# Products of keys, scores and carried keys split into 64-column halves in one stretch, and the result turned behind the third token product

## What is computed

```
z = cumlogsumexp(s);  g = exp(z_prev - z);  p = exp(s - z)
hk = hk * g + k (x) p;   ok = q @ hk;   pv = softmax(ok)      # one 64x64 state per head
hv = hv * g + p (x) v;   ov = pv @ hv                         # one 64x128 state per head
o  = ov * rsqrt(mean(ov^2) + eps) * g_norm * silu(x @ Wg);  out = o @ Wo
```

## Time and profile before

| | |
|---|---|
| median of 3 runs | 1312.45 us (1312.39 to 1312.88) |
| the profiled execution | 1312.18 us, span 1310.5 us |
| TensorE busy | 1301.9 us, 99% |
| VectorE, ScalarE, GpSimd busy | 71%, 41%, 33% |
| a cell, from the turn of `k` to the next (cell 13, 474.92 to 510.50 us) | 35.58 us |

### The profile page before, as it was taken

One profiled execution on the slowest core, in us unless ns is written; L12 is line 12 of the kernel. 1 busy time (PEld: TensorE's weight loads), 2 busy tenths in 40 slices (PEclk: granted clock), 3 DMA queues, 4 the chain that ended last, 5 costly groups with the idle time before them and its releaser, 6 DMA issues.

```text
span 1310.5 us, 21956 instructions
## 1 busy us (share of the span) xinstructions
PE 1301.9 (99%) x8644; PEld 1150.5 (88%) x8644; DVE 934.2 (71%) x1887; ACT 534.5 (41%) x1551; POOL 426.4 (33%) x390
## 2 busy tenths in 40 slices
PE   9999999999999999999999999999999999999998
PEld 7888888888988888888888888888888898988886
DVE  6777777777777777777777677777777777767654
ACT  5634443344334443444334434444334434632221
POOL 4412342154223431234225422343123413442211
PEclk9999999999999999999999999999999999999999
DMA  7002100010000100010001000010000110000000
GB/s 239 27 33 82 33 17 2 1 57 17 1 1 25 33 17 2 25 33 17 1 1 55 8 13 2 25 33 18 1 25 25 65 34 1 1 1 33 33 33 33
DMA packets 20023, 36.04 MB, mean 28 GB/s; under 512 B 3024, under 2 KB 3024, under 8 KB 19920
## 3 DMA queue, kind: packets, MB, share of 16 engines
q1 hardware_dynamic: 19920, 34.63, 8.1%
HBM read 30.43 MB, written 4.19 MB: 26 GB/s over the span
## 4 chain that ended last, share of the span: by engine, by line
PE 99%; DVE 1%; issue 0%; ACT 0%; POOL 0%; POOLq 0%; DVEq 0%
PE p L1059 15%; PE p L1060 15%; PE p L1061 15%; PE t L1144 5%; PE o L1328 3%; PE s L1212 3%; PE xb L1281 3%; PE p L1212 2%; PE o L1264 2%; PE t L1328 2%; PE o L1266 2%; PE s L1155 2%; PE s L1636 2%; PE s L1156 2%; PE s L1157 2%; PE s L1637 2%
## 5 line engine op out<-in xcount | busy, mean ns | idle before, releaser
L1059 PE MATMUL p<-wvg_hi,xt_hi 128*128 128x512 f32 x508 | 201.5, 397 | 0.0
L1060 PE MATMUL p<-wvg_lo,xt_hi 128*128 128x512 f32 x508 | 198.5, 391 | 0.0
L1061 PE MATMUL p<-wvg_hi,xt_lo 128*128 128x512 f32 x508 | 197.9, 390 | 0.0
L554 POOL TENSOR_TENSOR orstd<-ovar,minus_half 128x8 f32<-128x8 f32 x32 | 52.4, 1637 | 424.8 <-DVE ovar L1010 424.8
L516 POOL TENSOR_TENSOR s_lo<-sums,s_hi 128x512 fp32r<-128x512 f32 x64 | 83.0, 1298 | 225.9 <-ACT s_hi L645 225.9
L1059 PE MATMUL p<-xt_hi,wsqk_hi 128*128 128x512 f32 x376 | 149.4, 397 | 0.0
L1060 PE MATMUL p<-xt_lo,wsqk_hi 128*128 128x512 f32 x376 | 146.9, 391 | 0.0
L1061 PE MATMUL p<-xt_hi,wsqk_lo 128*128 128x512 f32 x376 | 146.6, 390 | 0.0
L620 ACT ACTIVATE v_tok<-p 128x256 f32<-128x256 f32 x128 | 49.6, 387 | 220.8 <-PE p L1061 217.8
L908 DVE COPY hv<-xb 64x128 f32<-64x128 f32 x192 | 55.1, 287 | 89.4 <-PE xb L1281 88.1
L1061 PEld LDWEIGHTS p<-wvg_hi,xt_lo 128*128 128x128 f32 x508 | 95.4, 188 | 20.7
(11 more groups left out here) (284 smaller groups left out, 3549.9 us busy)
## 6 DMA issues: line engine op xcount, KB each, us to landing
raw<-in_Wvg SPq DMA_DIRECT2D x32, 256.0 KB, 2.7
raw<-in_Wsqk SPq DMA_DIRECT2D x24, 256.0 KB, 2.7
raw<-in_L_attn_Wo SPq DMA_DIRECT2D x16, 256.0 KB, 2.9
acc<-in_x SPq DMA_DIRECT2D x4, 1024.0 KB, 5.7
out<-acc SPq DMA_DIRECT2D x16, 256.0 KB, 2.0
acc<-in_x_turned SPq DMA_DIRECT2D x3, 1024.0 KB, 8.8
acc<-in_x_turned SPq DMA_DIRECT2D x4, 256.0 KB, 4.1
v_raw<-in_L_ffn_V SPq DMA_DIRECT2D x1, 1024.0 KB, 5.5
```

The costliest lines, as they stand in the source:

```text
L554: nc.gpsimd.tensor_tensor(orstd[:], ovar[:], minus_half[:], ALU.pow).then_inc(orstd_done, 1)
L1059: nc.tensor.matmul(out_, lh, rh, start=(k == 0), stop=False)
L1060: nc.tensor.matmul(out_, lh, rl, start=False, stop=False)
L1061: last = nc.tensor.matmul(out_, ll, rh, start=False, stop=(k == n - 1))
```

## The change

1. `running_keys`, the scores' products and the carried keys' products are made per head, with 64 columns of weights and the result in its own 64 partitions of the bank. The products of `ok` are swapped: `e_tok` and `hk` are now the weights and `ws_t` and `q_t` move, so `ok` comes out with slots on partitions.
2. They stand in one stretch. The turns of `rz_t` are gone, both turns of `y` stand ahead of it.
3. `ok` is scaled by `rz_t` (`okt`), turned by TensorE behind token product 2 into the bank `s1`, and VectorE reads it there for the largest and the subtraction. `pz` is turned unscaled, and VectorE scales it by `rz_t` on the way to `pz_t`. ScalarE's copies to `rz_tok` and `pz_t` are gone.
4. On VectorE `add_m24(1)` and `add_m1` still stand behind the subtraction. ScalarE and GpSimd make `e_tok_hi`, `e_tok_lo` and `v_lo` ahead of the parts of `sums`.

```diff
@@ cell_tensor
-                nc.tensor.matmul(XB[:, 0:P], k_tok[:, c, :], e_tok[:, c, 1:3, :].rearrange("p h m -> p (h m)"),
-                                 start=(c == 0), stop=True, skip_group_check=True).then_inc(hk_summed, 1)
+                for h in range(2):
+                    mm = nc.tensor.matmul(XB[h * DK:(h + 1) * DK, h * M:(h + 1) * M], k_tok[:, c, h * DK:(h + 1) * DK],
+                                          e_tok[:, c, 1 + h, :], start=(c == 0), stop=True, skip_group_check=True)
+                mm.then_inc(hk_summed, 1)
+            def slots_of_scores(c):
+                for h in range(2):
+                    nc.tensor.matmul(OB[h * M:(h + 1) * M, tokens(c)], e_tok[:, c, 1 + h, :], ws_t[:, c, h, :],
+                                     start=(c == 0), stop=True, skip_group_check=True)
+            def slots_of_carried(c):
+                pe.wait_ge(hk_kept, cell.count(CH - 1, c))
+                for h in range(2):
+                    mm = nc.tensor.matmul(OB[h * M:(h + 1) * M, tokens(c)], hk[:, c - 1, h * M:(h + 1) * M],
+                                          q_t[:, tokens(c)], start=False, stop=True, skip_group_check=True)
...
             token_proj(pe, cell, 2)
+            pe.wait_ge(ok_scaled, cell.count(1, 1))
+            turned(OK_BANK, [okt[:, tokens(c)] for c in range(CH)], ok_turned)
             running_values(0)
...
-            pe.wait_ge(pz_done, cell.count(1, 1))
-            turned(PZ_BANK, [pz[:, c, :, :].rearrange("p h m -> p (h m)") for c in range(CH)], pz_turned)
+            pe.wait_ge(exp_done, cell.count(1, 1))
+            turned(PZ_BANK, [ok[:, c, :, :].rearrange("p h m -> p (h m)") for c in range(CH)], pz_turned)
@@ cell_vector
+            if not first(cell):
+                y_sums(dve, cell, 0)
+                add_m24(dve, cell, 0)
+                y_sums(dve, cell, 1)
             dve.wait_ge(ok_summed, cell.count(1, 1))
+            nc.vector.tensor_tensor(okt[:], OB[:], rz_t[:], ALU.mult).then_inc(ok_scaled, 1)
+            dve.wait_ge(ok_turned, cell.count(1, 1))
+            nc.vector.tensor_reduce(top[:], by_token, AX_X, ALU.max).then_inc(top_done, 1)
...
+            nc.vector.tensor_tensor(groups, by_token,
                                     top[:].rearrange("p (g a) -> p g a", a=1).broadcast_to([P, 2 * CH, M]),
                                     ALU.subtract).then_inc(ok_less_top, 1)
...
                 add_m24(dve, cell, 1)
                 add_m1(dve, cell)
...
+            dve.wait_ge(pz_turned, cell.count(1, 1))
+            nc.vector.tensor_tensor(pz_t[:], PZ_BANK[:], rz_t[:], ALU.mult).then_inc(pz_t_done, 1)
```

More of the change, by code:

```diff
@@ L297, in attention @@
         k_tok = sb("k_tok", [P, CH - 1, P])
[L298 removed]
+        okt = sb("okt", [P, T])
         hk = sb("hk", [P, CH - 1, P])
         ok = sb("ok", [P, CH, 2, M])
[L301 removed]
+        rz_t = sb("rz_t", [P, T])
         v_tok = sb("v_tok", [P, CH, VW])
@@ L533, in cell_gpsimd @@
             for c in range(CH - 1):
-                if c == 1 and not first(cell):
+                if c == 2 and not first(cell):
+                    sums_low(pool, cell.shifted(-1), 0)
                     sums_low(pool, cell.shifted(-1), 1)
@@ L659, in cell_scalar @@
                                  ACT.Copy).then_inc(k_tok_done, 1)
+            act.wait_ge(e_tok_done, cell.count(1, 1))
+            slots_high(act)
             if J is not None:
@@ L682, in cell_scalar @@
                 y_high(act, cell, 1)
[L683 to L686, removed]
+            values_high(act, cell, 0)
             values_high(act, cell, 1)
             if not first(cell):
+                sums_high(act, cell, 0)
                 sums_high(act, cell, 1)
@@ L823, in y_low, with y_sums @@
                                     ALU.subtract).then_inc(yt_lo_done, 1)
-        def y_sums(dve, cell, half, meanwhile=None):
+        def y_sums(dve, cell, half):
             prev = cell.shifted(-1)
@@ L1244, in cell_tensor @@
             pe.wait_ge(k_tok_done, cell.count(1, 1))
-            running_keys(0)
-            pe.wait_ge(rz_done, cell.count(1, 1))
-            turned(RZ_BANK, [rz_t[:, tokens(c)] for c in range(CH)], rz_turned)
             if not first(cell):
                 turned_y(pe, cell, 0)
-            running_keys(1)
-            pe.wait_ge(scores_masked, cell.count(2, 2))
-            for c in range(CH):
-                if c == 2 and not first(cell):
-                    pe.wait_ge(rz_tok_done, cell.count(1, 1))
-                    turned_y(pe, cell, 1)
-                if c == 2:
-                    running_keys(2)
-                o = OB[:, c * P:(c + 1) * P]
-                if c > 0:
-                    pe.wait_ge(hk_kept, cell.count(CH - 1, c))
-                    nc.tensor.matmul(o, q_t[:, tokens(c)], hk[:, c - 1, :], start=True, stop=False)
-                nc.tensor.matmul(o.rearrange("p (h m) -> p h m", h=2), ws_t[:, c, 0, :], e_tok[:, c, 1:4:2, :],
-                                 start=(c == 0), stop=False)
-                mm = nc.tensor.matmul(o.rearrange("p (h m) -> p h m", h=2), ws_t[:, c, 1, :], e_tok[:, c, 0:3:2, :],
-                                      start=False, stop=True)
+                turned_y(pe, cell, 1)
+            running_keys(0)
+            pe.wait_ge(scores_masked, cell.count(2, 2))
+            slots_of_scores(0)
+            slots_of_scores(1)
+            running_keys(1)
+            slots_of_scores(2)
+            slots_of_scores(3)
+            running_keys(2)
+            slots_of_carried(1)
+            slots_of_carried(2)
+            mm = slots_of_carried(3)
             mm.then_inc(ok_summed, 1)
```

50 lines of the change are left out of this document (15 added, 35 removed).

## The result

| | before | changed | |
|---|---|---|---|
| median | 1312.42 us (1312.37 to 1312.88, 4 runs) | 1375.29 us (1374.86 to 1375.49, 4 runs) | ratio 1.0477 [1.0464, 1.0489] |
| span of the profiled execution | 1310.5 us | 1373.6 us | +63.1 us |
| a plain cell | 35.59 us | 37.28 us | +1.69 us |

The change makes the kernel 4.8% slower; 1378 us were forecast. The cells are measured from the first turn product of `k` to the next cell's; "plain" are those in the middle that repeat to 0.1 us, which leaves out cells 0, 1 and 31, and in some kernels 2 and 30.

A forecast was written before the change was run, and what follows sets the result against it. TensorE, busy 99% of the span, was taken to bound the kernel; 31 * (0.06 + 2.01) = 64.2 plus 1.0 in cell 0 on 1312.18 gave 1377.4, with 0.27 to the median 1378 us; range 1364 to 1418.

The forecast's parts named there:

- The wait: TensorE stands still within rows_second for add_m1, queued on VectorE behind the late turn of ok: 2.01 us in each cell.
- The stretch: TensorE's run of products that makes ok: 4.05 us against 4.43, so -0.38; with the turn of ok +0.06 per cell.
- the chain: Keys' products waiting for VectorE's kept states: three links of 0.75 and the last carried pair set 2.65 to 2.98, taken 2.8.
- the switches: TensorE going between whole array and halves around the stretch: 0.19 each way, 0.38 together.
- Side by side: Column halves in the stretch run side by side: 0.056 a product, 40 products together 2.24, or 1.90.
- start 0.112 apart: Sign in the trace that the prediction is wrong: the products with 128 moving columns start 0.112 apart.
- The rule of the Trainium skill: Rival: loads and products of column halves don't overlap, so the stretch's products take 7.6 instead of 2.8; 1527 us, chance 0.02.
- in turn: Rival: the column halves run one after the other in the stretch, +1.2 a cell, 1415 us; chance 0.15.
- The edges: In cell 0 the late top stands ahead of the kept values that running_values(1) needs: 1.0 us (0 to 2).
- The clock: Rival: TensorE's clock falls in the new pauses, 2.5 more a cell, 1455 us; chance 0.04.
- a clock row that isn't full: Sign in the changed trace that the prediction is wrong: the clock row isn't full.
- No second wait: VectorE's lateness adds no further TensorE wait, counted 0; rival: one on t0 or kept values, 0.6 a cell, 1397, chance 0.06.

The follow-up runs named there:

- e1: The changed kernel with add_m24(1) and add_m1 moved ahead of VectorE's wait for ok_turned, nothing else; 1310.55 us, ratio to before 0.9979.
- e2: The changed kernel with add_m24(1) and add_m1 between top and the subtraction; 1352.44 us, ratio 1.0301.
- e8: The changed kernel with add_m24(1) and add_m1 moved further back, behind the sum of the exponentials; 1450.34 us, ratio 1.1044.
- e7: e1 with groups of f32 products that feed nothing, in cell 0 ahead of the keys' products, on halves or whole array; one run, 1327.06 us.
- e5: e1 with the first keys' product on the whole array ahead of the turns of y and the next keys' products each one step earlier; 1297.47 us.
- e6: e5 with operations moved in the cells that carry extra work (0, 1, 2, last), on ScalarE and VectorE; 1290.84 us, ratio 0.9833.

## Why the prediction was right

**The wait (right, 2.01 forecast, 2.10 measured).** It stands where it was put, 31 times, released by `add_m1`. The path from the turn was 3.27 (3.25), TensorE's cover 1.17 (1.24). e1 removes the cause and gives the 2.08 back. e2 takes one step of VectorE out (0.73 less of pause, 0.75 less of a cell), e8 puts a step and the wait for ScalarE in (1.4 and 1.39 more), and the time follows. That the adds read PSUM made no difference, as taken.

**The stretch (right in kind, mis-sized).** -0.38 was forecast, -0.81 measured: 3.62 instead of 4.05. The term that was mis-sized is the chain. I had links of 0.75 with a further 0.06 to 0.17 each for the keys' own pair ahead of them; start to start a link is 0.73, keys' pair included. Three links of 0.73 and the last carried pair's 0.22 are 2.41 where I took 2.8; the switches are the rest, 0.33, where I took 0.38, and e7 alone gives 0.14 and 0.20 for them. The gap ahead of a keys' product is some 0.1 (the last score's record begins at 545.45, 0.27 ahead of the end of its row, and takes 0.11; the next keys' product starts at 545.67), where I had named 0.3. That the chain and not the products sets the length is shown by e5 and e6: a link taken out shortens the stretch by 0.42, although the products on the array cost no less (the first keys' pair of 0.17 became a whole-array one of 0.22).

**Side by side (right).** Pairs of halves with 128 moving columns cost 0.11, in the stretch (eight in the row of 0.61 at 545.11) and alone. The 0.056 that I took for one product is half of such a pair. The sign "start 0.112 apart" was badly put: on each half they do start 0.11 apart, and what the rival needed is that the two halves don't do so at the same time. The rule of the Trainium skill that I had weighed ("TensorE: Matmul & The Clock Gate", part 3: a load overlaps a running product only with another row group) would have made this 7.6 us instead of 2.4; e7's column halves have the same 128 rows (128*64 in its rows) and run side by side, so here the measurement decides against it. The rival "in turn" is false for the same reason. Its price was right, though: alone on its half a product with 128 moving columns costs 0.112, not 0.056, so had the halves not run side by side it would have come true in full.

**The edges (mis-sized).** For cell 0 1.0 was taken, 1.7 measured. The wait is the one that was named, for the kept values that `running_values(1)` needs: the view of TensorE's waits has it as

```profile
PE xb L1274 <- DVE hv L895: 1.4, 1, 1.4
```

and it stays in e1, where `top` is as late. TensorE also waits once for the kept keys (`hk`, 0.7), which I had not named. The 0.65 ahead of cell 0 is scatter. Cell 1 and cell 31 with what follows, 4.77 together against 2 * 1.66 for two plain cells, I had not priced apart. e1 still has such losses with the pause gone, and e6 removes most of them, cell 1's above all, by moving other operations. So there it is not the wait for `add_m1` but operations that stand ahead of a needed one in that cell only.

**The clock (a rival at 0.04, true in part).** I had named a fall in the new pauses and priced it at 2.5 a cell in every cell. It came in five cells, at 1.57 each: 7.9 us. The sign that I had named for it, a clock row that isn't full, did not show it: the slices are too wide. "No second wait" held: every other wait of TensorE stands once in the whole trace, none in each cell.

**The sum.** Forecast over the span 65.2, measured 63.2. The difference: 31 cells at 1.66 instead of 2.07, -12.7; the clock, +7.9; ahead of cell 0, +0.65 (scatter); cell 0, +0.7; cells 1 and 31, +1.45. That is -2.0; the rest is rounding and the distance between one execution and the median. That the errors nearly cancel is luck: taken singly, the stretch was off by its own size.

## What to carry to other kernels

Behind a wait for a late result, an in-order engine should have nothing queued that others need: the whole loss of this change was two independent adds on the wrong side of one wait, and moving them, with no other edit, turned 1375 into 1310.6. Halves of the array save time where many small products stand in a row, but the saving arrives only as far as the dependency chain through another engine is covered: here the halves were worth 0.4 us a cell once the turn of `ok` was paid, and starting the chain earlier as much again. After a reordering read the first and the last cells on their own: in e1 they cost some 9 us that no plain cell shows, and three moves won 6.6 of it back.

## What the runs showed of the hardware

- Column halves of the array ran as if each had its own queue: a product for the free half started 0.10 us (128 columns) and 0.43 us (512 columns) ahead of the last one of the group issued before it on the busy half.
- A switch from the whole array to halves cost 0.14 us and one back 0.20 in f32 (e7).
- The granted clock fell from 2.4 to 1.2 GHz behind recorded pauses of 1.84 us in 5 cells of 31, behind 3.2 us in 22 of 31, behind 1.1 us in no plain cell, and once each behind the single waits of 2.7 us (e1) and 2.6 us (e2) in cell 1. Why it was every sixth cell in the changed kernel (falls at 254.67, 479.95, 705.23, 930.51 and 1155.79 us, 225.28 apart) and not the others with the same pause was not tried and stays open.
- In f32 a product of 64 columns of weights and 128 moving costs 0.11 alone on its half, as much as a whole-array one: narrowing the weights pays only through the other half, or with 64 moving columns (0.058).
